# Mixture of experts on one core: rows turned behind the up products, four output buffers, the last three experts' down products placed sooner

## The reference

```python
xn = _layernorm(x, axis=-1)                       # x: 8192 tokens of 512
x = x + attn(xn) + ffn(xn)                        # attn: random features, dense
# ffn, E = 64 experts, CAP = 256 slots each, K = 8 of 64 chosen per token in the best 4 of 8 groups
dispatch = zeros(E, CAP, 512).at[flat_e, pos_c].add(tokens[tidx] * valid)
g = einsum('ech,ehi->eci', dispatch, gate_w)      # 512 -> 256
u = einsum('ech,ehi->eci', dispatch, up_w)        # 512 -> 256
expert_out = einsum('eci,eih->ech', silu(g) * u, down_w)   # 256 -> 512
output = zeros(t, 512).at[tidx].add(expert_out[flat_e, pos_c] * weight * valid)
output = output + (silu(tokens @ sg) * (tokens @ su)) @ sd
```

## Time and profile before

| | us |
|---|---|
| median of 3 runs (1302.28 to 1361.43) | 1304.08 |
| the profiled execution | 1302.23 |
| its span | 1300.5 |
| PE busy | 1281.0 (98% of the span) |
| DVE, ACT, POOL busy | 913.4, 650.3, 441.9 |

### The profile page before, as it was taken

How to read it: one execution, slowest core, us unless ns; L and a number is a source line. 1 busy time by engine, 2 the same in 40 slices (tenths; PEclk the granted TensorE clock), 3 DMA queues, 4 the chain that set the end, 5 groups by cost and what they waited for, 6 DMA issues and landing times.

```text
span 1300.5 us, 22607 instructions
## 1 busy us (share of the span) xinstructions
PE 1281.0 (98%) x7585; PEld 1126.6 (87%) x7585; DVE 913.4 (70%) x1787; ACT 650.3 (50%) x1061; POOL 441.9 (34%) x344
## 2 busy tenths in 40 slices
PE   8999999999999999999999999999999999999995
PEld 7888888888888888888889999999999999999994
DVE  7887787867878678775556667666766666676662
ACT  6422223222232222322256777777777777777772
POOL 2000000000000000000014667766766776676663
PEclk9999999999999999999999999999999999999998
DMA  9246554466544665435448999999999999999995
GB/s 319 73 136 168 136 129 101 137 167 145 119 102 136 167 145 119 102 104 136 136 132 250 270 289 288 291 289 288 293 280 292 286 292 294 290 284 290 291 277 65
DMA packets 202776, 263.65 MB, mean 203 GB/s; under 512 B 49268, under 2 KB 137208, under 8 KB 202744
## 3 DMA queue, kind: packets, MB, share of 16 engines
q1 hardware_dynamic: 173272, 191.40, 50.7%
q0 software_dynamic: 28672, 71.32, 23.8%
q10 hardware_dynamic: 800, 0.53, 0.2%
HBM read 178.18 MB, written 71.39 MB: 192 GB/s over the span
## 4 chain that ended last, share of the span: by engine, by line
PE 97%; DMA 1%; POOL 0%; DVE 0%; issue 0%; ACT 0%
PE pmm L1268 18%; PE pmm L1266 18%; PE pmm L1267 18%; PE pout L1266 11%; PE pout L1268 11%; PE pout L1267 11%; PE ptr L1504 4%; PE plp L1331 2%; DMA out_dram<-outs,slot_cols 1%; PE plp L1360 1%; PE plp L1340 1%; POOL out_dram L1630 0%; PE ptr L1278 0%; PE pout L1453 0%; DVE proj_lo L809 0%
## 5 line engine op out<-in xcount | busy, mean ns | idle before, releaser
L1630 POOL DMA_INDIRECT out_dram<-outs,slot_cols x128 | 227.1, 1774 | 157.8 <-DMA out_dram<-outs,slot_cols 123.1
L1266 PE MATMUL pmm<-xt_hi,proj_hi 128*128 128x256 f32 (+1 forms) x776 | 249.6, 322 | 0.6 <-DVE xt_lo L809 0.6
L1268 PE MATMUL pmm<-xt_hi,proj_lo 128*128 128x256 f32 (+1 forms) x776 | 246.6, 318 | 0.0
L1267 PE MATMUL pmm<-xt_lo,proj_hi 128*128 128x256 f32 (+1 forms) x776 | 246.6, 318 | 0.0
L1266 PE MATMUL pmm<-xt_hi,sgu_hi 128*128 128x256 f32 (+1 forms) x768 | 246.1, 320 | 0.2 <-issue 0.2
L1267 PE MATMUL pmm<-xt_lo,sgu_hi 128*128 128x256 f32 (+1 forms) x768 | 243.4, 317 | 0.0
L1268 PE MATMUL pmm<-xt_hi,sgu_lo 128*128 128x256 f32 (+1 forms) x768 | 243.4, 317 | 0.0
L1614 POOL TENSOR_TENSOR earlier<-earlier,chosen 128x64 bf16<-128x64 bf16 x64 | 24.2, 379 | 609.9 <-DVE chosen L930 606.2
L1620 POOL DMA_INDIRECT xbuf<-rows,slot_cols x128 | 183.3, 1432 | 82.7 <-issue 38.3
L555 ACT ACTIVATE feat<-pmm,ab 128x512 f32<-128x512 f32 x66 | 45.4, 688 | 286.5 <-PE pmm L1268 286.5
L1267 PEld LDWEIGHTS pmm<-xt_lo,proj_hi 128*128 128x128 f32 x776 | 147.8, 190 | 10.2
(11 more groups left out here) (196 smaller groups left out, 2561.2 us busy)
## 6 DMA issues: line engine op xcount, KB each, us to landing
raw<-in_L_ffn_gate_w_dram SPq DMA_DIRECT2D x64, 512.0 KB, 6.8
raw<-in_L_ffn_up_w_dram SPq DMA_DIRECT2D x64, 512.0 KB, 8.9
raw<-in_L_ffn_down_w_dram SPq DMA_DIRECT2D x64, 512.0 KB, 6.1
outs<-in_L_attn_x_dram SPq DMA_DIRECT2D x32, 512.0 KB, 3.9
out_dram<-outs SPq DMA_DIRECT2D x32, 512.0 KB, 3.1
xbuf<-in_L_attn_x_dram SPq DMA_DIRECT2D x52, 256.0 KB, 7.5
raw<-xn SPq DMA_DIRECT2D x52, 256.0 KB, 6.2
rows<-raw SPq DMA_DIRECT2D x39, 256.0 KB, 4.2
```

What stands on the lines that cost most here:

```text
L1266: pe.matmul(psum, lh, rh, start=first and n == 0, stop=False)
L1267: pe.matmul(psum, lh, rl, start=False, stop=False)
L1268: ins = pe.matmul(psum, ll, rh, start=False, stop=final and n == len(pairs) - 1)
L1630: pool.indirect_dma_start(out=out, out_offset=bass.IndirectOffsetOnAxis(ap=slot_cols[:, at:at + 1], axis=0), in_=outs[e.b][:, c, :], in_of ...
```

## The change

Three things. (1) Inside a stage PE turns the next expert's rows behind the up products, `e_gate_up(e)`, `e_turn(e+1)`, `e_down(e-1)`, and the other engines follow: ACT starts a stage with silu, and in the third stage of a chunk (`looked`) makes the up half of `gate_up_hi` last; DVE starts with the gate half of `gate_up_lo`, then `e_hidden`, then `e_turned_lo`. The turned rows are split in two halves with a semaphore step each, and `slot_weights` waits for the transposes and no longer for ACT. PE's gate products wait for `silu_done` and its up products for `e_hid_made`. SP loads gate and up of expert n ahead of down of n-1. The first matmul of each expert's gate products is 64 columns wider (`E_LEAD`); the extra columns hold nothing that is used. (2) Four output buffers: `feat` and the free ends of `xbuf` join `outs`, so `e_out(e)` waits for the adds of `e-4`. (3) At the end, `e_down(61)` stands between gate and up products of expert 62, `e_down(62)` between those of 63, and the last expert's hidden values and down products are made in two halves, the second half of its up products lying in `ptr`.

The diff, with unchanged lines partly left out; left out whole are `e_last_hidden` and `e_last_hidden_lo` on DVE, which do the multiplication and the split for one half of 256 columns each:

```diff
@@ -56,6 +56,7 @@
+E_LEAD = 64
@@ -207,6 +208,8 @@
+        e_outs = [[t[:, c, :] for c in range(CB)] for t in (outs[0], outs[1], feat)]
+        e_outs.append([xbuf[c][:].rearrange("p j h -> p (j h)")[:, CB * ROW:CB * ROW + H] for c in range(CB)])
@@ -222,6 +225,7 @@
+        last_up = ptr[:, 0, 0:CAP]
@@ -521,27 +525,32 @@
-            def refill(e):
...
-                b = e.b
+            def refill_gate_up(e):
...
-                    load_half(b, m, source[e.n])
+                    load_half(e.b, m, source[e.n])
...
+            def refill_down(e):
...
-                load_down(b, down_w[e.n])
...
-            sp.wait_ge(edn_lo_made, 1)
-            load_down(0, down_w[2])
-            refill(turn(3))
+                load_down(e.b, down_w[e.n])
...
+            refill_gate_up(turn(3))
+            refill_down(turn(2))
...
-                    refill(Turn(2 * m + 2 + k // 2, k % 2, k // 2))
+                    e = Turn(2 * m + 2 + k // 2, k % 2, k // 2)
+                    refill_gate_up(e)
+                    refill_down(e.prev())
...
-                refill(turn(n))
+                refill_gate_up(turn(n))
+                refill_down(turn(n - 1))
+            refill_down(turn(E - 1))
@@ -730,8 +739,10 @@
             def e_turned_hi(e):
-                act.wait_ge(e_turned, e.n + 1)
-                act.activation(xt_hi[e.b][:, :, E_COLS], ptr_e, copy).then_inc(e_xt_hi_made, 1)
+                for half in range(2):
+                    at = slice(2 * half, 2 * half + 2)
+                    act.wait_ge(e_turned, 2 * e.n + half + 1)
+                    act.activation(xt_hi[e.b][:, at, E_COLS], ptr_e[:, at], copy).then_inc(e_xt_hi_made, 1)
             def e_silu(e):
@@ -743,38 +754,63 @@
+            def e_last_hidden_hi(e, i):
+                act.wait_ge(e_hid_made, e.n + i + 1)
+                act.activation(hid_hi[:, e.b, i, :], hid[:, i * CAP:(i + 1) * CAP], copy).then_inc(e_hid_hi_made, 1)
...
             def e_out(e):
...
-                at_least(act, added, 16 * CB * (e.n - 1))
+                at_least(act, added, 16 * CB * (e.n - 3))
...
-                    act.activation(outs[e.b][:, c], pout[c], copy, scale=slot_w[e.q][:, c:c + 1]).then_inc(
+                    act.activation(e_outs[e.q][c], pout[c], copy, scale=slot_w[e.q][:, c:c + 1]).then_inc(
...
-            def stage(e, next_rows=True, next_weights=True, out_prev=True, look=None):
+            def stage(e, next_rows=True, next_weights=True, out_prev=True, look=None, first=False,
+                      looked=False):
+                e_silu(e)
+                if next_weights:
+                    gate_up_hi(e.next(), (0,) if looked else (0, 1))
...
-                if next_weights:
-                    gate_up_hi(e.next())
-                e_silu(e)
-                down_hi(e)
...
+                if looked:
+                    gate_up_hi(e.next(), (1,))
+                if first:
+                    for b in range(2):
+                        act.wait_ge(out_stored[b], 16 * GROUPS)
+                if not next_rows:
+                    down_hi(e)
...
+                if next_rows:
+                    down_hi(e)
...
-            for b in range(2):
-                act.wait_ge(out_stored[b], 16 * GROUPS)
-            stage(turn(1))
-            with act.Fori(0, CHUNKS - 2) as m:
+            stage(turn(1), first=True)
+            def chunk(m):
...
-                    stage(four(2 * m + 1, k), look=m + 2 if k == 1 else None)
-            for n in range(E - 6, E - 1):
+                    stage(four(2 * m + 1, k), look=m + 2 if k == 1 else None, looked=k == 2)
...
+            chunk(0)
+            with act.Fori(1, CHUNKS - 2) as m:
+                chunk(m)
+            for n in range(E - 6, E - 2):
...
-            stage(turn(E - 1), next_rows=False, next_weights=False)
+            e_silu(turn(E - 2))
+            e_turned_hi(turn(E - 1))
+            gate_up_hi(turn(E - 1))
+            e_out(turn(E - 3))
+            down_hi(turn(E - 2))
+            e_hidden_hi(turn(E - 2))
+            e_silu(turn(E - 1))
+            down_hi(turn(E - 1))
+            e_out(turn(E - 2))
+            for i in range(IB):
+                e_last_hidden_hi(turn(E - 1), i)
@@ -1216,10 +1252,14 @@
             def e_turned_lo(e):
-                dve.wait_ge(e_xt_hi_made, e.n + 1)
+                dve.wait_ge(e_turned, 2 * e.n + 2)
...
-                dve.tensor_tensor(xt_lo[e.b][:, :, E_COLS], ptr_e, xt_hi[e.b][:, :, E_COLS].bitcast(F32),
-                                  ALU.subtract).then_inc(e_xt_lo_made, 1)
+                for half in range(2):
+                    at = slice(2 * half, 2 * half + 2)
+                    dve.wait_ge(e_xt_hi_made, 2 * e.n + half + 1)
+                    dve.tensor_tensor(xt_lo[e.b][:, at, E_COLS], ptr_e[:, at],
+                                      xt_hi[e.b][:, at, E_COLS].bitcast(F32),
+                                      ALU.subtract).then_inc(e_xt_lo_made, 1)
             def e_hidden(e):
@@ -1228,6 +1268,19 @@
+            def e_last_hidden(e, i):
+                dve.wait_ge(silu_done, e.n + 1)
+                dve.wait_ge(e_up_done, e.n + i + 1)
+                dve.wait_ge(e_hid_hi_made, e.n)
+                dve.wait_ge(e_hid_lo_made, e.n)
+                at = slice(i * CAP, (i + 1) * CAP)
+                dve.tensor_tensor(hid[:, at], gate_t[:, at], (pmm[1][:, at], last_up)[i], ALU.mult).then_inc(e_hid_made, 1)
...
+            def e_last_hidden_lo(e, i):
+                dve.wait_ge(e_hid_hi_made, e.n + i + 1)
+                dve.tensor_tensor(hid_lo[:, e.b, i, :], hid[:, i * CAP:(i + 1) * CAP],
+                                  hid_hi[:, e.b, i, :].bitcast(F32), ALU.subtract).then_inc(e_hid_lo_made, 1)
...
             def e_hidden_lo(e):
@@ -1235,35 +1288,47 @@
                                   ALU.subtract).then_inc(e_hid_lo_made, 1)
 
             def stage(e, next_rows=True, next_weights=True, look=None):
+                if next_weights:
+                    gate_up_lo(e.next(), (0,))
+                e_hidden(e)
                 if next_rows:
                     e_turned_lo(e.next())
                 if next_weights:
-                    gate_up_lo(e.next())
-                e_hidden(e)
+                    gate_up_lo(e.next(), (1,))
+                e_hidden_lo(e)
                 down_lo(e)
-                e_hidden_lo(e)
                 if look is not None:
                     look[0](look[1])
 
             e_turned_lo(turn(0))
             output(turn(GROUPS - 1), 3)
-            stage(turn(0), next_weights=False)
+            e_turned_lo(turn(1))
+            stage(turn(0), next_rows=False, next_weights=False)
             stage(turn(1))
             with dve.Fori(0, CHUNKS - 2) as m:
                 for k in range(CHUNK):
                     stage(four(2 * m + 1, k), look=(pass_blocks, None, slot_tokens, None)[k] and (
                         (pass_blocks, None, slot_tokens, None)[k], m + 2))
-            for n in range(E - 6, E - 1):
+            for n in range(E - 6, E - 2):
                 stage(turn(n))
-            stage(turn(E - 1), next_rows=False, next_weights=False)
+            e_turned_lo(turn(E - 1))
+            gate_up_lo(turn(E - 1))
+            e_hidden(turn(E - 2))
+            down_lo(turn(E - 2))
+            e_hidden_lo(turn(E - 2))
+            down_lo(turn(E - 1))
+            for i in range(IB):
+                e_last_hidden(turn(E - 1), i)
+                e_last_hidden_lo(turn(E - 1), i)
 
 
         @block.tensor
         def _(pe):
-            def products(psum, pairs, first=True, final=True):
+            def products(psum, pairs, first=True, final=True, lead=False):
 
                 for n, (lh, ll, rh, rl) in enumerate(pairs):
-                    pe.matmul(psum, lh, rh, start=first and n == 0, stop=False)
+                    if n > 0 or not lead:
+                        pe.matmul(psum, lh, rh, start=first and n == 0, stop=False)
                     pe.matmul(psum, lh, rl, start=False, stop=False)
                     ins = pe.matmul(psum, ll, rh, start=False, stop=final and n == len(pairs) - 1)
                 return ins
@@ -1498,25 +1563,53 @@
             def e_turn(e):
...
-                at_least(pe, e_xt_lo_made, e.n)
+                at_least(pe, e_xt_lo_made, 2 * e.n)
...
-                ins.then_inc(e_turned, 1)
+                    if h % 2 == 1:
+                        ins.then_inc(e_turned, 1)
             def e_gate_up(e, parts=(0, 1)):
-                pe.wait_ge(e_xt_lo_made, e.n + 1)
-                at_least(pe, e_hid_made, e.n)
+                pe.wait_ge(e_xt_lo_made, 2 * (e.n + 1))
...
+                    if m == 0:
+                        at_least(pe, silu_done, e.n)
+                    else:
+                        at_least(pe, e_hid_made, e.n)
...
-                        ins = products(pmm[m][:, i * CAP:(i + 1) * CAP], [
+                        lead = m == 0 and i == 0
+                        if lead:
```

(43 more changed lines are left out.)

## The result

The changed kernel takes **1299.21 us** in the median of 20 runs (1297.67 to 1305.47), the kernel before 1303.48 (20 runs). The ratio is 0.9958, 95% interval 0.994 to 0.9976: a gain of 4.3 us, or 0.4%. The forecast was 1305.6, a loss of 1.5. The time lies in the range (1298 to 1319) and far within 2%, but the sign was wrong. The profiled execution took 1298.49, its span is 1296.8.

The account below looks back on a forecast made before the run. PE, tight until its end, then POOL's chain of landing adds bound the kernel. Span 1281.9 + 3.6 + 16.5 = 1302.0, 1.5 above before; added to the median 1304.08 this gave 1305.6 us, range 1298 to 1319.

Parts of the forecast that it names:

- The wider matmul: First gate matmul of each expert on PE, 64 columns wider: costs 28 ns in 64 stages, 1.7 us, lower end 0.
- a period more than 0.05 from 9.28: Sign of being wrong: PE's stage, from transposes to transposes, differs from 9.28 us by more than 0.05.
- Rival (b): The 0.08 us lost on PE at the turn from transposes to products disappears 64 times: 1297 us, chance 0.05.
- the junction loss: About 0.08 us lost on PE between transposes and next products; claimed to move with the transposes, counted as nothing.
- Waits in a plain stage: In ordinary expert stages nothing waits; the next gate products' rows have 1.1 us to spare.
- Waits behind a look-up: PE narrowly waits for xt_lo after each of 14 look-ups: 0.13 us each, 1.8 us in all, between 0 and 18.
- The end: After the last up product, POOL's chain of landing adds ends 16.5 us later instead of 18.6: a gain of 2.1.
- Four buffers: Four output buffers free ACT of waits of 1.0 us in all, off PE's path: worth 0.
- Rival (d): Adds on POOL bound every stage if their cycle exceeds 9.4 us: 1336 us; chance 0.05, shared with another rival.
- The block on POOL: Gathers beside DVE instructions with two SBUF inputs get blocked; by this rule all the end's gain but 0.9 us goes.

Follow-up runs that it names:

- no_lead: The changed kernel with its first gate matmul back at 256 columns, all else kept: 1304.56 us, ratio 1.0012 to the kernel before.
- experiment 5: The changed kernel with two output buffers again in place of four: 1301.92 us, ratio 0.9987 to the kernel before.
- split_signs: The changed kernel with ACT's eight sign sums split, four in a chunk's second stage and four late in the third: 1312.49 us.
- wide_loads: The changed kernel with gate and up weights loaded in 4 KB pieces, not 1 KB, transposes reading every fourth column: 1332.3 us.
- experiment 8: The changed kernel with smaller load pieces: down weights only 1301.25 us, all weights 1300.41; with ACT's sign sums also split, 1302.34 and 1294.12.
- small_all: The changed kernel with down weights loaded in 1 KB pieces and gate and up weights in 512 byte pieces: 1300.41 us, ratio 0.9963.

## Why the prediction was wrong, and where it was right

**The wider matmul: this step failed.** It was entered as 28 ns of cost in each of 64 stages, "1.7, with 0 as the lower end". Its own cost was right (0.147 us until the next start, 0.029 more than 0.118). What failed is the lower end: I let the matmul cost something or nothing, and didn't ask what it does to the 47 behind it. They follow each other in 113.8 ns in place of 117.9, and in the end it was worth -5.3 us (`no_lead` against the changed kernel) in place of +1.7. A stage of 9.13 us is also what the prediction had named as a sign of being wrong, a period more than 0.05 from 9.28. The condition under which this could have been seen was named, "if a 256-column matmul is held by its weight load"; I then only freed the extra columns by it. A row of before even had the fast spacing: right behind PE's short idle time at 692.03 us the matmuls stood 113.4 ns apart, and I looked at none of them.

**Rival (b)** gave 1297, near the measured time and for the wrong reason: the junction loss did not go away (0.32 from the first to the second down matmul), it moved, as the forecast had it.

**Waits in a plain stage: right.** No engine makes PE wait in one.

**Waits behind a look-up: right in kind, too small.** `xt_lo` was forecast at 9.30 behind the first gate matmul; the stage's next one starts at 1027.52 - 1018.20 = 9.32. But PE was faster than assumed, so the gap is 0.18 and not 0.13, the next matmul starts 0.1 late as well, and 3 of the 14 stages that start with it lost the fast spacing. Taking it away gave 4.5 us where adds don't bind, against the 1.8 entered.

**The end: right in shape, wrong in its start.** T, the end of the last up product, was put at 1285.5 and came at 1277.5; the end of the span followed 19.3 us later and not 16.5. That the time still fell into the range is thus partly two errors against each other. All four last pairs wait for landings, the last outputs were ready ahead of their pair (by 4.8 us, not 3), part 3 gave nothing in the trace. But the gain of 2.1 us from an earlier start of that chain did not come: its pair 60 starts 17.4 us ahead of the last output's completion (1264.07 to 1281.46), where the prediction had T - 17.2 and T + 3.1, which is 20.3 us. It assumed that adds(59) follow their gather at once; they were waiting for the landing of adds(58), as all adds now do. End less last output: 1296.8 - 1281.46 = 15.3 us, 14.9 before, 13.4 forecast. The three last steps took 22.2 us, not the 23.16 that were carried over from before.

**Four buffers: 0 isn't refuted.** They were costed by ACT's waits before (1.0 us). With adds 8 to 10 us behind two buffers make ACT wait (experiment 5); at the lag of the changed kernel the medians leave room for 0 and for a few us.

**Rival (d)**, adds as the bound of every stage, did not come true at 9.13 to 9.6 us a stage, but it was close: 0.3 us less in one stage of four set it off (`split_signs`), and so did larger load pieces (`wide_loads`, at 1332; the prediction had priced the rival at 1336). The cycle of the adds, from which by the prediction it decides above 9.4 us, is 9.28 us in the mean in the changed kernel, 9.63 in the trace of `split_signs` and 9.74 in that of `wide_loads`, and there the lag of the adds grows as described.

**The block on POOL.** The gathers in their new place take 1342 ns in the mean, 1432 before. The rule quoted in the prediction from the Trainium skill ("SBUF — State Buffer", "Who interferes with whom") did not make them longer on the whole. The block itself is in both traces: from 700 us on gathers that share less than 0.05 us with a DVE instruction of two SBUF inputs take 1.06 us before (13 of 118) and 1.09 after (5 of 119), the others 1.50 and 1.37 in the mean. It was there in the old place too. What held POOL was the landing.

For that the DMA queues matter. With gate and up weights in pieces of 4 KB a packet of POOL's queue took 185 ns, with 512 bytes 168. The Trainium skill ("DMA: Bandwidth & Descriptors", "Queues, rings and completion order") says that a DMA engine takes turns between the queues that have work, and switches only when it has drained a packet. With all adds the traces agree in direction: the larger the pieces of the one queue, the longer a packet of the other takes. With half of the adds they show no difference, and they don't show how many pieces one turn has.

**Left open.** Why a matmul wider by 64 columns behind 512-column ones sets off the faster spacing, why a delayed start sometimes does, and why it then lasts for 47 matmuls: the runs show the condition for stages that start without a delay, and not the mechanism. Nor is it the only condition: the 24 up products of the first expert before, from 688.00 us on, follow transposes without a delay or a wide matmul, and stand 113.7 ns apart. Open too is by what small pieces help, beyond the times of experiment 8.

## What to carry to other kernels

An edit that lengthens one instruction can change the pace of all that follow it without a gap: compare starts over a whole group, in every place of the trace where the group follows something else, before you enter only its own length. When two chains are nearly equally long, cost a gain on the first against the slack of the second; here the adds had 3 to 5 us of lag, and taking 0.3 us out of one stage of four cost 13 us in the median (9 without its six longest runs). And where a queue whose steps wait for landings shares the DMA engines with bulk loads, try the loads in smaller pieces: it made a 1312 us kernel a 1294 us one, though it raised the engines' busy share.

## What the hardware showed that I had not expected

- A stream of 256-column float32 matmuls has two paces, 117.7 to 118 and 113.4 to 114 ns, at the same granted clock of 1.00. In stages that start without a delay a first matmul of 320 columns directly behind 512-column ones gives the faster (46 of 46); one of 256 or 272 columns (0 of 46 each), or of 320 behind transposes (0 of 60), doesn't. Behind a delayed first matmul either came, whatever its width (11, 7 and 6 of 14 fast with 320, 256 and 272 columns).
- Transposes that read every fourth column take 0.89 us for eight, against 0.80.
- Loads in pieces of 4 KB in place of 1 KB made the kernel 29 us slower than the one before; 26 of its loss against the changed kernel appear only with all adds there. Pieces of 512 bytes cost the loads' queue more engine time (57.1% in `small_all` against 50.8%) and the kernel nothing that its runs tell.
